# Layer one of a message network inside the stage that counts its edges

## The chip, the cores and the metric

The kernel runs on one core of a Trainium2 chip. Its time is the device time in microseconds (us) of one execution. A core has TensorE (PE in the profile; PEld are its weight loads), VectorE (DVE), ScalarE (ACT), GpSimd (POOL) and SyncE (SP). SP and ScalarE issue the DMAs here, each on a queue of its own.

## The reference, cut to what matters

```python
# N = 3125 nodes, E = 100000 edges sorted by dst, D = 128, 200 relations
deg = jnp.maximum(segment_sum(ones, dst, N), 1.0)
norm = deg ** (-0.5)
h = jnp.maximum(_layernorm(x), 0.0)
for W_r, W_sl, W_el in ((W_r1, W_sl1, W_el1), (W_r2, W_sl2, W_el2)):
    self_msg = jnp.where(isolated[:, None], h @ W_el, h @ W_sl)
    agg = segment_sum((rel_embed[rel_id] + h[src]) @ W_r, dst, N)
    h = rrelu(agg * norm + self_msg)         # slope 0.229 below zero
x = x + h
h = jnp.maximum(_layernorm(x), 0.0)
x = x + graph_attention(h, src, dst, ...)    # softmax over the edges of a node
```

## The kernel before, in words

**Counts instead of edges.** The kernel never gathers rows by edge. It builds `counts`: 27 planes of 3125 target columns. Plane j (0 to 24) holds in row p how many edges lead from node 125j + p to each target; planes 25 and 26 hold the same for the two halves of the relations. A segment sum of h over edges is then a dense product of h with `counts`. Nodes come in 25 blocks of 125.

**Counting, `build_counts`.** The edges are cut into 800 tiles of 125, and four tiles make a group, 200 groups in all. Edges are sorted by target, so a group touches a narrow window of columns only. The groups come in 60 batches (`BATCHES`): 20 of four groups, then 40 of three, with a window width per tile from 2 to 17. For each batch VectorE writes one-hot matrices into one of two halves of a ring: `lo` at line 353, then two builds at line 357. TensorE multiplies them (lines 397 and 399: four tiles of a group, into one of four pairs of PSUM banks) and adds a carried column (line 405, the "carry"). ScalarE takes the next carry out of PSUM (lines 448, 450) and copies the window into `counts` at a column read from a register (line 456); each 20 groups it loads 20 such registers. The last product of a batch frees its ring half (`ring_free`). VectorE waits for the half that TensorE freed, TensorE for `ring_ready`, for its PSUM banks (`put`) and for the carry. Beside it x is normalised in five pieces (statistics on VectorE, the power on GpSimd, lines 261 to 264, the scaling on ScalarE, line 464) and sent to memory as h.

**Checks, `check_counts`.** A stage of its own: degrees by one-column products (line 542), the norm, a check that the columns assumed were right, with a slow second path if not, and the relation rows split into three bf16 parts.

**Layers, `message_layer`.** Twice. First h is split in pieces of five blocks into three bf16 parts (ScalarE lines 871 and 873, VectorE 913 and 915). Then come 13 chunks of two target blocks (the last has one). Per chunk: `own` turns the chunk's own h (line 803), `sums` multiplies 25 blocks by three parts with 250 columns of counts (line 813) and six relation parts (line 816), ScalarE takes both out (877, 879), `weigh` multiplies with the self weights (832) and with W_r (836), ScalarE scales (885) and VectorE finishes (927, 933, 939). Layer two also adds x, stores it, normalises, stores h3, turns it and makes the query rows (lines 822, 841). The last chunk of layer two stores through SP, behind the reload of h3 for attention (lines 757 to 770).

**Attention** follows, and every part (`nc.Block`) ends with a barrier of all engines.

## Time and profile before

| | us |
|---|---|
| median of 3 runs (901.11 to 901.99) | 901.21 |
| the profiled execution | 901.91 |
| its span, first to last instruction | 899.9 |
| counting, to the last window | 0 to 288.6 |
| degrees, checks | 288.6 to 305 |
| layer one | 305 to 446.3 |
| layer two | 446.3 to 591.9 |
| nothing busy | 591.9 to 603.9 |
| attention | 603.9 to 899.9 |

The stages are read from the timeline; the bounds are where TensorE starts or ends the stage's work. The other 2.0 us lie around the span. Busy times are sums over instructions that may overlap on an engine, so an engine near 100% is its stage's limit and one at 60% isn't, unless somebody waits for it each time.

### The profile page before, as it was taken

What the parts mean: (1) busy time and instruction counts of PE and PEld (TensorE: products, weight loads), DVE (VectorE), ACT (ScalarE), POOL (GpSimd) and SP (SyncE); (2) the same over time, 40 slices, a digit from 0 to 9 for tenths busy, and PEclk for the clock granted to TensorE, in tenths of its full rate; (3) what the DMA queues carried; (4) which work ended last, traced back from release to release, by engine and by line L of the source; (5) the groups of instructions that cost most, each with busy time, mean ns of one, the idle gap of its engine ahead of it and who ended that gap; (6) DMA issues with size and microseconds to landing.
All of it is one profiled execution on the core that took longest, in us unless ns stands there. A gap on an engine that the chain in (4) does not pass through costs nothing. (4 is left out here: it accounts for less than half of the span.)

```text
span 899.9 us, 16551 instructions
## 1 busy us (share of the span) xinstructions
PE 740.8 (82%) x5767; PEld 552.3 (61%) x5767; DVE 529.8 (59%) x947; ACT 424.2 (47%) x1019; POOL 242.2 (27%) x248
## 2 busy tenths in 40 slices
PE   4466665666666599999799999929999999999994
PEld 3456555655656498888789999814444444444463
DVE  4998989899996411111343333313458585867677
ACT  0555666567666311111221111117767676767661
POOL 3054920000000000000000000005657666666662
PEclk6555789899899699999899999959999999999996
DMA  4000000000001000000001111120000000000000
GB/s 117 10 3 29 28 17 2 2 2 1 1 1 59 28 1 0 0 0 0 21 19 34 34 37 37 34 91 19 0 1 7 17 9 14 15 10 20 4 23 17
DMA packets 22080, 17.20 MB, mean 19 GB/s; under 512 B 1122, under 2 KB 20224, under 8 KB 22024
## 3 DMA queue, kind: packets, MB, share of 16 engines
q1 hardware_dynamic: 21804, 16.09, 6.1%
q8 instruction: 31, 0.51, 0.2%
q10 hardware_dynamic: 220, 0.40, 0.1%
q14 instruction: 25, 0.20, 0.1%
HBM read 10.09 MB, written 6.40 MB: 18 GB/s over the span
## 5 line engine op out<-in xcount | busy, mean ns | idle before, releaser
L397 PE MATMUL sums<-work 125*128 125x196 f16 (+15 forms) x1220 | 159.2, 265 | 66.6 <-DVE work L357 66.5
L813 PE MATMUL l_ps_g<-counts,work 125*128 (+2 forms) x1950 | 209.0, 269 | 0.6 <-DVE work L915 0.6
L813 PEld LDWEIGHTS l_ps_g<-counts,work 125*128 125x128 bf16 x1950 | 184.9, 99 | 19.0 <-DVE work L915 1.1
L1178 POOL TENSOR_TENSOR counts<-counts,work 125x500 f32<-125x500 f32 x150 | 162.3, 1082 | 97.5 <-DVE work L1242 84.1
L1101 PE MATMUL a_ps_o<-work 125*128 125x500 f32 (+1 forms) x350 | 159.6, 547 | 7.1 <-DVE work L1246 6.1
L1089 PE MATMUL a_ps_s<-work 128*125 128x500 f32 x300 | 152.9, 592 | 12.4 <-PEq L732 12.4
L1242 DVE SCALAR_TENSOR_TENSOR work<-a_ps_s,counts 125x500 f32<-125x500 f32 x150 | 101.5, 677 | 95.0 <-ACT a_ps_s L1198 94.9
L397 PEld LDWEIGHTS sums<-work 125*128 125x128 f16 x1220 | 103.1, 112 | 72.8 <-DVE work L357 71.6
L1193 ACT ACTIVATE a_ps_s<-a_ps_s,work 125x500 f32<-125x500 f32 (+1 forms) x157 | 102.1, 650 | 91.8 <-PE a_ps_s L1089 88.7
L399 PE MATMUL sums<-work 125*128 125x10 f16 (+15 forms) x800 | 138.3, 201 | 0.0
L456 ACT CAST counts<-sums 128x364 f32 (+38 forms) x305 | 130.9, 467 | 8.3 <-issue 1.3
L353 DVE TENSOR_TENSOR work<-work 125x3024 f16<-125x3024 f16 (+1 forms) x60 | 114.1, 1902 | 20.0 <-PE sums L399 18.3
L357 DVE TENSOR_TENSOR work<-work 125x4200 f16<-125x4200 f16 (+15 forms) x120 | 125.4, 1087 | 0.0
L927 DVE SCALAR_TENSOR_TENSOR work<-l_ps_s,small,work 125x128 f32<-125x128 f32 x50 | 15.3, 347 | 171.3 <-ACT work L885 171.3
L1101 PEld LDWEIGHTS a_ps_o<-work 125*128 125x128 f32 x350 | 64.4, 196 | 76.6 <-issue 67.3
L1089 PEld LDWEIGHTS a_ps_s<-work 128*125 128x125 f32 x300 | 55.9, 190 | 78.1 <-issue 78.1
L879 ACT COPY work<-l_ps_g 128x250 f32<-128x250 f32 (+1 forms) x26 | 9.4, 360 | 196.0 <-PE l_ps_g L816 196.0
L1198 ACT ACTIVATE a_ps_s<-a_ps_s,work 125x500 f32<-125x500 f32 (+1 forms) x157 | 100.7, 642 | 0.0
L786 POOL MEMSET work<- 125x1 f32 x1 | 0.1, 98 | 325.3 <-POOLq L732 325.3
L399 PEld LDWEIGHTS sums<-work 125*128 125x128 f16 x800 | 85.6, 108 | 1.6
L405 PE MATMUL sums<-work,ident_h 128*128 128x14 f16 (+2 forms) x305 | 41.3, 187 | 32.0 <-ACT work L448 17.2
L405 PEld LDWEIGHTS sums<-work,ident_h 128*128 128x128 f16 x305 | 25.8, 110 | 38.6 <-ACT work L448 19.8
(157 smaller groups left out, 625.2 us busy)
## 6 DMA issues: line engine op xcount, KB each, us to landing
counts<-in_x SPq DMA_DIRECT2D x5, 312.5 KB
h_nodes<-counts SPq DMA_DIRECT2D x5, 312.5 KB
work<-h_nodes SPq DMA_DIRECT2D x5, 312.5 KB
work<-in_x SPq DMA_DIRECT2D x12, 125.0 KB
x_after_messages<-work SPq DMA_DIRECT2D x12, 125.0 KB
h_attention<-work SPq DMA_DIRECT2D x12, 125.0 KB
work<-h_attention SPq DMA_DIRECT2D x2, 750.0 KB
counts<-x_after_messages SPq DMA_DIRECT2D x12, 125.0 KB
```

Source lines behind the costliest of these rows:

```text
L353: dve.tensor_tensor(lo[:, 0:t * 2 * LO].rearrange("p (t c two) -> p t c two", c=LO // 2, two=2), iota_h[:, None, 0:LO].rearrange("p o (c t ...
L357: last = dve.tensor_tensor(out.rearrange("p t (c two) -> p t c two", two=2), iota_h[:, None, 0:c].rearrange("p o (c two) -> p o c two", tw ...
L397: pe.matmul(win[:, 0:c, cols], lo[:, k * 2 * LO:k * 2 * LO + 128], m[:, k, h0 * w:(h0 + c) * w].rearrange("p (h d) -> p h d", d=w), start= ...
L399: last = pe.matmul(win[:, c:, cols], lo[:, (2 * k + 1) * LO:(2 * k + 1) * LO + 128], r[:, k, :].rearrange("p (h d) -> p h d", d=w), start= ...
L456: act.copy(counts[:, h0:h1, bass.ds(at0, c)], buf[:, i, 0:(h1 - h0) * span].rearrange("p (h d) -> p h d", d=span)[:, :, 0:c]).then_inc(put ...
L813: pe.matmul(ps_g[:, 0:nb * NP], parts[:, j, s, :], counts[0:NP, j, cols], start=j == 0 and s == 0, stop=False)
L1089: last = pe.matmul(out[0:NP, :WIDE], qk_t[:, j * NP:(j + 1) * NP], qk_t[:, c * WIDE:(c + 1) * WIDE], start=True, stop=True)
L1101: last = pe.matmul(ps_o[c % 2][:, 0:cols(u) // n], h3[:, j + i, :], pbuf[u % PB][:, i * NP:i * NP + cols(u) // n], start=j + i == 0, stop= ...
L1178: pool.tensor_tensor(a, a, p, ALU.add).then_inc(acc_done, 1)
L1193: act.activation(s, s, ACT.Relu, bias=five, scale=-float(D) ** -0.5).then_inc(limited, 1)
L1198: act.activation(s, s, ACT.Exp, bias=five, scale=-1.0).then_inc(exped, 1)
L1242: dve.scalar_tensor_tensor(pbuf[u % PB], ps_s[u % 4][0:NP, 0:WIDE], float(np.exp(-CLIP)), counts[0:NP, j, c * WIDE:(c + 1) * WIDE], ALU.ma ...
```

## The change

`build_counts`, `check_counts` and the two calls of `message_layer` become one function, `messages`, in one block. Since the edges are sorted, the first 250 columns of `counts` are final once a certain group is put, and so on: `READY` lists that group for each of the 13 chunks. `plan` gives layer one's steps to slots, a slot being the place between a group's one-hot products and its carry. Chunk 0 begins at group 72, chunk c at `READY[c]` + 3: `own` there (with the degrees of the chunk), eight source blocks (24 matmuls) in each of the next three slots, the last block with `self` and `rest` in the fourth, `agg` two slots on. The chunks begin at 72, 85, 103, 118, 131, 143, 154, 165, 174, 183 and 192; the last two (11 and 12) run behind group 199. The PSUM ring of counting has three pairs of banks, the fourth serves layer one.

To make room, x, the three parts of h and the keys of the one-hot matrices lie in columns of `counts` that aren't counted yet, and move when counting comes near: after chunk 1 SP stores columns 0 to 499 of 25 planes to memory (`heads`), moves late keys and later the parts there, and brings the columns back after the last chunk. h of layer one goes to memory (`store`), and comes back for chunks 0 to 9; chunks 10 to 12 stay. The norm is a power on GpSimd per chunk. The checks move into counting, with new ones that every chunk's columns are final when assumed. Layer two runs its chunks in the order 2 to 11, 1, 0, 12, unrolled. At its end x and h3 of the last chunk are stored from ScalarE's queue, the reload of h3 has six pieces, and attention waits for each piece only where it needs it.

```diff
-             "flag": sb("flag", [1, 1], I32)}
-        T["h3"] = view(T["work"], 4 * N, NP, NB * D, F32)
-        T["hn_in"] = [ctx.enter_context(nc.semaphore(f"hn_in{i}")) for i in range(5)]
-        T["h3_in"] = [ctx.enter_context(nc.semaphore(f"h3_in{i}")) for i in range(3)]
-        build_counts(nc, ctx, T, src, dst, rel, x, h_dram)
-        T["wts1"] = ctx.enter_context(nc.semaphore("weights1_in"))
-        T["rel_step1"] = ctx.enter_context(nc.semaphore("rel_step"))
-        check_counts(nc, ctx, T, src, dst, rel, rel_embed, w_r1, w_sl1, w_el1)
-        message_layer(nc, ctx, T, 1, None, None, None, {})
-        message_layer(nc, ctx, T, 2, w_r2, w_sl2, w_el2, {"x": x, "x2": x2, "h3": h3, "wqk": wqk, "bqk": bqk})
...
+LB = 2
+CHUNKS = -(-NB // LB)
+READY = (58, 82, 100, 115, 128, 140, 151, 162, 171, 180, 189, 197, 200)
+FIRST_SLOT = 72
+AT_ONCE = 8
...
+    for c in range(CHUNKS):
+        s0 = FIRST_SLOT if c == 0 else READY[c] + 3
+        s1 = READY[c + 1] + 1 if c + 1 < CHUNKS else GROUPS
+        s0, s1 = min(s0, GROUPS), min(s1, GROUPS)
+        slots[s0].append(("own", c, 0))
+        for j in range(NB):
+            slots[min(s0 + 1 + j // AT_ONCE, GROUPS)].append(("sum", c, j))
+        s1 = min(s0 + 1 + NB // AT_ONCE, GROUPS)
+        slots[s1].append(("self", c, 0))
+        slots[s1].append(("rest", c, 0))
+        slots[min(GROUPS, s1 + 2)].append(("agg", c, 0))
+    at = {}
+    for g, steps in enumerate(slots):
+        for kind, c, j in steps:
+            at[kind, c] = g
+    assert all(at["agg", c] <= at["own", c + 1] for c in range(CHUNKS - 1))
+    return slots, at
+
...
-            sp.wait_ge(h_out, 16 * 5)
-            sp.wait_ge(ring_free, len(BATCHES) - 1)
-            for i in range(5):
-                sp.dma_start(hn[0:NP, 5 * D * i:5 * D * (i + 1)], h_dram[:, 5 * D * i:5 * D * (i + 1)]).then_inc(T["hn_in"][i], 16)
+            def store(c):
+                sp.wait_ge(y_done, c + 1)
+                sp.dma_start(h1_dram[:, c * LB * D:(c + 1) * LB * D], t1.rearrange("p b f -> p (b f)")).then_inc(h1_out, 16)
+
+            store(0)
+            store(1)
+            sp.wait_ge(sums_done, 2)
+            sp.wait_ge(put, 2 * READY[1])
+            for i in range(5):
+                v = slice(5 * i, 5 * i + 5)
+                sp.dma_start(heads.rearrange("p (j d) -> p j d", d=HEAD)[:, v, :], counts[0:NP, v, 0:HEAD]).then_inc(put_out, 16)
+            sp.wait_ge(put_out, 16 * 5)
+            for b in range(MOVED, len(BATCHES), 4):
+                i = b - MOVED
+                got = counts[0:NP, key_plane(b), KEY_AT:KEY_AT + 8 * KEY_TILES].rearrange("p (a s e) -> p s a e", a=2, s=4)
+                for a in range(2):
+                    sp.dma_start(counts[0:NP, i:i + 4, 3 * D + 48 * a:3 * D + 48 * a + 48], got[:, :, a, :]).then_inc(keys_moved, 16)
+            store(2)
+            for i in range(5):
+                v = slice(5 * i, 5 * i + 5)
+                sp.dma_start(counts[0:NP, v, 0:3 * D], counts[0:NP, v, PART_AT:PART_AT + 3 * D]).then_inc(parts_moved, 16)
+            for c in range(3, DIRECT):
+                store(c)
+            sp.wait_ge(ring_free, len(BATCHES))
+            sp.wait_ge(h1_out, 16 * DIRECT)
+            for i, (j0, j1) in enumerate(PIECES2[:4]):
+                sp.dma_start(hn[0:NP, j0 * D:j1 * D], h1_dram[:, j0 * D:j1 * D]).then_inc(hn_in[i], 16)
+            sp.wait_ge(sums_done, CHUNKS)
+            for i in range(5):
+                v = slice(5 * i, 5 * i + 5)
+                sp.dma_start(counts[0:NP, v, 0:HEAD], heads.rearrange("p (j d) -> p j d", d=HEAD)[:, v, :]).then_inc(heads_in, 16)
...
+                again_sp(sp)
+                sp.wait_ge(R["parts2"], 10)
+
+
+            sp.wait_ge(put, 2 * GROUPS)
+            sp.wait_ge(agg_done, CHUNKS)
+            for t, v in zip((wr, ws[:, 0:D], ws[:, D:]), weights2):
+                sp.dma_start(t, v).then_inc(L["wts"], 16)
+            sp.dma_start(wqk, wqk_d).then_inc(L["wts"], 16)
+            sp.dma_start(bqk, bqk_d.rearrange("(p o) -> p o", o=1)).then_inc(L["wts"], 16)
+            sp.dma_start(x_last, by_block(x, LAST)).then_inc(L["last_in"], 16)
+            sp.wait_ge(y_done, CHUNKS)
+            for i, c in enumerate(ORDER2[:-1]):
...
-                    if g < 4:
-                        pe.wait_ge(later_keys, 3 * (g + 1))
-                    else:
-                        pe.wait_ge(put, 2 * (g - 3))
+            def layer1(kind, c, j):
+                nb = blocks_of(c)
+                p = parts1(c)
+                cols = cells(c)
+                w = nb * NP
+                if kind == "own":
+                    pe.wait_ge(put, 2 * READY[c])
+                    if c:
+                        pe.wait_ge(agg_out, c)
+                    else:
+                        pe.wait_ge(outside_set, 3)
+                        pe.wait_ge(flagged, 1)
+                        pe.wait_ge(rest1[1], 1)
+                    if c == HEAD_CHUNK:
+                        pe.wait_ge(parts_moved, 16 * 5)
+                    for b in range(nb):
+                        for s in range(3):
+                            pe.matmul(ps1[:, h_at + b * NP:h_at + (b + 1) * NP], p[:, c * LB + b, s, :], ident_h[0:NP, 0:NP], start=s == 0, stop=s == 2)
+                    for b in range(nb):
+                        k = c * LB + b
+                        for h in range(RH):
+                            last = pe.matmul(ps1[0:NP, 2 * h_at + b:2 * h_at + b + 1], counts[0:RL, NB + h, k * NP:(k + 1) * NP], ones_h,
+                                             start=h == 0, stop=h == RH - 1)
+                    last.then_inc(own_done, 1)
+                if kind == "sum":
+                    if j == 0:
+                        pe.wait_ge(ht_out, c + 1)
+                    if c == 0 and j % 5 == 0:
+                        pe.wait_ge(rest1[1], j // 5 + 1)
+                    for s in range(3):
+                        pe.matmul(ps1[:, 0:w], p[:, j, s, :], counts[0:NP, j, cols], start=j == 0 and s == 0, stop=False)
+                if kind == "self":
+                    if c == 0:
+                        pe.wait_ge(wts1, 16 * 3)
+                    else:
+                        pe.wait_ge(y_done, c)
+                    for b in range(nb):
+                        last = pe.matmul(ps2[0:NP, b * 2 * D:(b + 1) * 2 * D], ht[:, b * NP:(b + 1) * NP], ws, start=True, stop=True)
+                    last.then_inc(self_done, 1)
+                if kind == "rest":
+                    if c == 0:
+                        pe.wait_ge(rel_step, 6)
+                    for h in range(RH):
+                        for s in range(3):
+                            last = pe.matmul(ps1[:, 0:w], rel_parts[:, h, s, :], counts[0:RL, NB + h, cols], start=False, stop=h == RH - 1 and s == 2)
+                    last.then_inc(sums_done, 1)
+                if kind == "agg":
+                    pe.wait_ge(agg_out, c + 1)
+                    pe.wait_ge(self_taken, c + 1)
+                    for b in range(nb):
+                        last = pe.matmul(ps2[0:NP, b * D:(b + 1) * D], ht[:, b * NP:(b + 1) * NP], wr, start=True, stop=True)
+                    last.then_inc(agg_done, 1)
+
+            for b, (n, w) in enumerate(BATCHES):
...
-                with sp.Fori(1, FULL) as c:
-                    chunk(c, LB)
-                sp.wait_ge(summed, FULL + 1)
-                sp.wait_ge(h3_out, 16 * FULL)
-                reload(0, 0, 12)
-                reload(1, 12, FULL * LB)
-                chunk(FULL, NB - FULL * LB)
-                sp.wait_ge(h3_out, 16 * (FULL + 1))
-                reload(2, FULL * LB, NB)
-                sp.wait_ge(x2_out, 16 * (FULL + 1))
+            sp.wait_ge(L["summed"], CHUNKS)
+            sp.wait_ge(L["h3_out"], 16 * LAST)
+            for i, (j0, j1) in enumerate(T["h3_pieces"]):
+                if j0 == LAST * LB:
+                    sp.wait_ge(L["h3_last"], 16)
+                sp.dma_start(T["h3"][:, j0 * D:j1 * D], h3[:, j0 * D:j1 * D]).then_inc(T["h3_in"][i], 16)
+            sp.wait_ge(L["x2_out"], 16 * LAST)
+            sp.wait_ge(L["x2_last"], 16)
...
+                nb = blocks_of(c)
+                v = slice(c * LB, c * LB + nb)
+                w = nb * NP
+                ps1, ps2 = psum[:, 6, :], psum[:, 7, :]
+                if kind == "own":
+                    deg = ps1[0:NP, 2 * LB * NP:2 * LB * NP + nb]
+                    act.wait_ge(own_done, c + 1)
+                    act.activation(iso[:, v], deg, ACT.Relu, bias=1.0, scale=-1.0).then_inc(iso_set, 1)
+                    act.copy(degs[:, v], deg)
+                    if c:
+                        act.wait_ge(agg_done, c)
+                    act.copy(ht[:, 0:w], ps1[:, LB * NP:LB * NP + w]).then_inc(ht_out, 1)
+                    act.wait_ge(iso_set, 2 * c + 1)
+                    act.activation(some[:, v], iso[:, v], ACT.Identity, bias=1.0, scale=-1.0).then_inc(iso_set, 1)
+                if kind == "self":
+                    act.wait_ge(self_done, c + 1)
+                    act.wait_ge(iso_set, 2 * c + 2)
+                    if c:
+                        act.wait_ge(y_done, c)
+                        act.wait_ge(h1_out, 16 * min(c, DIRECT))
+                    for b in range(nb):
+                        k = c * LB + b
+                        both = ps2[0:NP, b * 2 * D:(b + 1) * 2 * D]
+                        act.mul(t2[:, b, :], both[:, 0:D], some[:, k:k + 1])
+                        last = act.mul(t1[:, b, :], both[:, D:], iso[:, k:k + 1])
+                    last.then_inc(self_taken, 1)
+                if kind == "rest":
+                    act.wait_ge(sums_done, c + 1)
+                    act.copy(ht[:, 0:w], ps1[:, 0:w]).then_inc(agg_out, 1)
+
...
+                if kind in ("own", "self", "rest"):
+                    layer1(kind, q)
+                    if kind == "own" and q == DIRECT + 1:
+                        for i in range(5):
+                            split(i)
+                    if kind == "rest" and q == DIRECT + 2:
+                        split(5)
+            split(6)
+            flag = act.alloc_register("again_act")
+            act.wait_ge(flagged, 1)
+            act.reg_load(flag, T["flag"][0:1, 0:1])
...
+            def ending(c):
+                nb = blocks_of(c)
+                dve.wait_ge(agg_done, c + 1)
+                dve.wait_ge(norm_set, c + 1)
+                if c:
+                    dve.wait_ge(y_done, c)
+                agg = psum[0:NP, 7, 0:LB * D].rearrange("p (b f) -> p b f", f=D)
+                for b in range(nb):
+                    k = c * LB + b
+                    dve.scalar_tensor_tensor(t1[:, b, :], agg[:, b, :], norm[:, k:k + 1], t1[:, b, :], ALU.mult, ALU.add).then_inc(y_step, 1)
+                done = LB * c + nb + c
+                dve.wait_ge(y_step, done)
+                t = t1[:, 0:nb, :]
+                dve.tensor_tensor(t, t, t2[:, 0:nb, :], ALU.add).then_inc(y_step, 1)
+                dve.wait_ge(y_step, done + 1)
+                out = t if c < DIRECT else hn_n[:, c * LB:c * LB + nb, :]
+                dve.scalar_tensor_tensor(out, t, SLOPE, t, ALU.mult, ALU.max).then_inc(y_done, 1)
+
+
...
-                dve.wait_ge(x2_out, c * 16 + 16)
-                dve.memset(rstd[0:1, 0:1], 1.0).then_inc(chunk_done, 1)
+                    rows(i - 1, ORDER2[i - 1])
+            act.wait_ge(L["x2_ready"], CHUNKS)
+            act.dma_start(by_block(x2, LAST), tmp[:, 0:1, :]).then_inc(L["x2_last"], 16)
+            late(LAST, LAST)
+            act.dma_start(h3[:, LAST * LB * D:], x_last.rearrange("p b f -> p (b f)")).then_inc(L["h3_last"], 16)
+            rows(LAST, LAST)
```

Three places in the order of instructions. TensorE, late in counting, between the last products of one group (lines 397, 399; 1021, 1023 after) and the first of the next: before,

```order
L397 MATMUL sums<-work 128x11x17
L399 MATMUL sums<-work 128x2x17
L405 MATMUL sums<-work,ident_h 128x14 [waits carry_ready]
L405 MATMUL sums<-work,ident_h 128x13
L397 MATMUL sums<-work 128x14x17 [waits put,ring_ready]
```

and after, at slot 193, the second slot of chunk 10:

```order
L1021 MATMUL sums<-work 128x11x17
L1023 MATMUL sums<-work 128x2x17
L982 MATMUL sums<-counts 128x250 [waits m_ht_out]
L982 MATMUL sums<-counts 128x250 x23
L1031 MATMUL sums<-work,ident_h 128x14 [waits carry_ready]
L1031 MATMUL sums<-work,ident_h 128x13
L1021 MATMUL sums<-work 128x14x17 [waits put,ring_ready]
```

The burst of 24 matmuls stands ahead of the carry, so ScalarE gets group 193's window later by the burst.

SP's queue from the last count to layer two's first loads: before (h back, then the weights of layer one, then those of layer two),

```order
L217 DMA work<-h_nodes 125x640 [waits ring_free,h_out]
...
L519 DMA work<-in_L0_gnn_rel_embed 100x2x128
L520 DMA work<-in_L0_gnn_W_r1 128x128
...
L737 DMA work<-in_L0_gnn_W_r2 128x128
...
L755 DMA work<-in_x 125x2x128
```

and after:

```order
L582 DMA work<-h_layer_one 125x640 [waits m_h1_out,ring_free]
L582 DMA work<-h_layer_one 125x640 x3
L586 DMA counts<-first_columns 125x5x500 [waits m_sums_done]
L586 DMA counts<-first_columns 125x5x500 x4
L601 DMA work<-in_L0_gnn_W_r2 128x128 [waits m_agg_done,put]
L601 DMA work<-in_L0_gnn_W_sl2 128x128
L602 DMA work<-in_L1_gnn_Wqk 128x128
...
L610 DMA work<-in_x 125x2x128 [waits m_y_done]
```

The return of the first 500 columns now stands in the queue between the last relation sums of layer one and the weights of layer two.

ScalarE behind the last group, after the change only (before, this order is in two blocks, all splits ahead of a layer's chunks):

```order
L1134 COPY work<-sums 128x250 [waits m_agg_done]
L1136 ACTIVATE small<-small 125x2 [waits m_iso_set]
L1212 CAST work<-work 125x5x128 [waits hn_in0]
...
L1212 CAST work<-work 125x5x128 [waits hn_in3]
...
L1212 CAST work<-work 125x2x128 [waits m_y_done]
L1146 ACTIVATE work<-sums,small 125x128 [waits m_y_done,m_h1_out,m_iso_set,m_self_done]
...
L1151 COPY work<-sums 128x250 [waits m_sums_done]
```

The first two rows and the last two belong to chunk 11; the splits of h for layer two (line 1212) stand between them.

## Rows read from the trace of the kernel before

**Rows 1.** Stretches: busy us (instructions) by engine, TensorE clock granted, DMA share, GB/s.

```profile
22.80:106.60 83.80, 49.92 (x648) 43.97 (x648) 77.27 (x125) 49.17 (x176) 37.21 (x17) 0.58 0.05 15
106.60:288.60 182.00, 115.40 (x1677) 106.96 (x1677) 164.44 (x124) 119.98 (x366) 10.85 (x4) 0.90 0.03 9
288.60:305.00 16.40, 5.68 (x52) 5.49 (x52) 4.98 (x18) 3.58 (x5) 0.00 (x0) 0.50 0.23 78
305.00:446.30 141.30, 135.82 (x1229) 121.00 (x1230) 28.67 (x74) 23.89 (x61) 0.10 (x1) 0.98 0.01 2
446.30:591.90 145.60, 140.82 (x1279) 126.95 (x1279) 56.84 (x210) 30.24 (x84) 8.94 (x13) 0.97 0.12 34
591.90:603.90 12.00, 0.00 (x0) 0.02 (x1) 0.06 (x1) 0.07 (x1) 0.03 (x1) 0.50 0.29 115
```

**Rows 2.** Who TensorE waited for, 22.8 to 288.6: us in total, times, longest.

```profile
PE sums L397 <- DVE work L357: 66.5, 46, 4.7
```

**Rows 3.** Timeline of VectorE: start, us, first build of a batch (widths 9, 17).

```profile
123.81 1.73 DVE L353 TENSOR_TENSOR work<-work 125x3024 f16<-125x3024 f16 x1
...
127.12 1.73 DVE L353 TENSOR_TENSOR work<-work 125x3024 f16<-125x3024 f16 x1
...
273.98 1.73 DVE L353 TENSOR_TENSOR work<-work 125x3024 f16<-125x3024 f16 x1
...
278.63 1.73 DVE L353 TENSOR_TENSOR work<-work 125x3024 f16<-125x3024 f16 x1
```

**Rows 4.** Timeline of TensorE: first products of two neighbouring groups, widths 8 and 17.

```profile
114.23 0.25 PE L397 MATMUL sums<-work 125*128 125x200 f16 x1
...
114.82 0.25 PE L397 MATMUL sums<-work 125*128 125x200 f16 x1
...
283.44 0.37 PE L397 MATMUL sums<-work 125*128 125x238 f16 x2 [1.66 <-DVE work L357]
...
284.40 0.27 PE L397 MATMUL sums<-work 125*128 125x238 f16 x1
```

**Rows 5.** Timeline of TensorE in layer one: the sums of two chunks in turn.

```profile
318.45 8.17 PE L813 MATMUL l_ps_g<-counts,work 125*128 x75
...
329.11 8.17 PE L813 MATMUL l_ps_g<-counts,work 125*128 x75
```

**Rows 6.** Timeline of VectorE: the ending of a chunk of layer one.

```profile
329.83 0.61 DVE L933 SCALAR_TENSOR_TENSOR work<-l_ps_a,small,work 125x128 f32<-125x128 f32 x2
330.60 0.42 DVE L939 SCALAR_TENSOR_TENSOR work<-work 125x256 f32 x1 [0.15 <-DVE work L933]
```

**Rows 7.** Timeline: registers reloaded at group 100, and the windows of one group late.

```profile
119.16 0.19 ACT L448 CAST work<-sums 128x27 f16 x1 [3.95 <-issue]
...
120.47 1.73 DVE L353 TENSOR_TENSOR work<-work 125x3024 f16<-125x3024 f16 x1 [2.69 <-PE sums L399]
...
286.16 1.09 ACT L456 CAST counts<-sums 128x504 f32 x2
```

**Rows 8.** Groups of instructions by line: busy us, mean ns of one, idle before.

```profile
L915 DVE TENSOR_TENSOR work<-work 125x640 bf16<-125x640 f32 x10 | 8.3, 826 | 7.9 <-ACT work L873 7.9
```

**Rows 9.** Timeline of TensorE: the last carry, and the first weighing of layer two.

```profile
286.24 0.20 PE L405 MATMUL sums<-work,ident_h 128*128 128x14 f16 x2
...
458.08 1.03 PE L832 MATMUL l_ps_s<-work 128*125 128x256 f32 x4
```

**Rows 10.** Timeline of GpSimd: two of its four steps on the scales of x.

```profile
102.64 11.33 POOL L261 TENSOR_SCALAR counts<-counts 125x5 f32<-125x5 f32 x1 [1.67 <-DVE counts L340]
114.05 1.20 POOL L262 TENSOR_TENSOR counts<-counts 125x5 f32<-125x5 f32 x1
```

**Rows 11.** Stretch while x arrives in pieces of 512 bytes: clock, DMA share, GB/s.

```profile
10.00:24.00 14.00, 0.50 0.37 97
```

**Rows 12.** Timeline at layer two's end: DMAs issued by SP, VectorE's last wait.

```profile
587.88 0.68 SPq L763 DMA_DIRECT2D work<-h_attention  x2
...
588.61 0.33 SPq L757 DMA_DIRECT2D x_after_messages<-work  x1
...
602.63 0.06 DVE L967 MEMSET work<- 1x1 f32 x1 [12.73 <-DMA x_after_messages<-work]
```

1165 lines of the change are left out of this document (642 added, 523 removed).

## The prediction

> **What bounds the kernel now.** I read the stages first, in the table of stretches [rows 1]. The learner is to see two kinds of stage. In the counting stage (22.8 to 288.6) VectorE is busy 92% and 90% of the time and TensorE 60% and 63%; nearly all of TensorE's longest waits there are for VectorE's one-hot batches, 66.5 us in all [rows 2]. In the two message layers (305 to 446.3 and 446.3 to 591.9) TensorE is busy 96% and 97%, VectorE 20% and 39%. Between them lie 16.4 us of counting degrees and checks, and 12.0 us before attention in which nothing computes at all. So layer one's matmuls would fit into TensorE's idle time only where that is large enough: it idles 182.0 - 115.4 = 66.6 us in the second part of counting, and layer one needs 12.5 times 10.66 us [rows 5]. That is the whole case: about 118 us of work go into a hole of 67 us, and what replaces the lost stage must be counted batch by batch.
>
> **Sum, part 1: counting up to group 72.** VectorE sets this pace and gets more to do. From the stage that goes away it takes the split of the relation rows (2.3 us of its 4.98 us of busy time in 288.6 to 305), and 8 of the 10 splits of h in pieces of five blocks (0.83 us each, as they take in the layers [rows 8], so 6.6 us), about 1.2 us of new checks, and up to 5 us for the 25 powers on GpSimd, done at once where five took 1.2 us [rows 10]; I take 2. ScalarE's norms and roundings come closer together (+1). Some of it falls into pauses VectorE has anyway (2.7 us at the worst one [rows 7]), -2. Sum +11 us, bounds 7 to 16. TensorE reaches group 72 at 117.7 instead of 106.7.
>
> **Part 2: groups 72 to 199.** A batch of three groups costs VectorE 3.31 us at width 9 and 4.65 us at width 17 [rows 3]; over the 42 batches that is 168 us, and pauses make it 180 (106.7 to 286.4). A group costs TensorE 0.59 us at width 8 and 0.96 us at width 17 [rows 4], 97 us in all by interpolation. Eleven of the thirteen chunks are placed here. A chunk is 10.66 us [rows 5], plus four one-column matmuls for the degrees, 118 us. Bare sums say TensorE 215 us, VectorE 168 plus eleven endings of 1.8 us (two steps at 0.61 a pair, two at 0.43 and the waits between them [rows 6]) = 188 us. But the one-hot ring holds one batch ahead only, so VectorE can't save up work during a burst: each batch costs the larger of the two. I added up the batches so. 23 of them hold bursts and are TensorE's: 55 us of counting and 107 us of layer one, and 28 us of waits that the change adds, 2.5 us a chunk: the turned h (ScalarE copies it after a carry of 0.2 us, evictions of 1.1 us for a group [rows 7] and two small steps, while TensorE has one group of 0.96 us to do), and the same way round before `agg`, where ScalarE has four products and a copy, 1.8 us, in front. The other 19 batches stay VectorE's: 83 us. Together 273 us. VectorE starts its next batch before the burst behind a batch's last group: -9. The reload of places each 20 groups (ScalarE silent 3.95 us, VectorE 2.69 [rows 7]) costs +5, since some fall into bursts. So 269 us for 180: +89, bounds +70 (no added waits) and +108 (4 us a chunk). Last group at 117.7 + 269 = 386 instead of 286.4: **+100 us** with part 1.
>
> **Part 3: from the last group to layer two's first products.** Before, the last count was done at 286.4 and the first `weigh` of layer two began at 458.1 [rows 9]: 171.7 us. After, two chunks are left, 10.7 and 6 us. ScalarE's order puts the splits 0 to 4 ahead of chunk 11's products: h comes back 12 us after the last group (1.28 MB; [rows 11] for the rate), and the last split ends at about +16, so `agg` of chunk 11 is at +18 and not +13, and the last relation sums are at +24. Own and sums of layer two (0.3 and 8.8 us) follow, ready to weigh at +35. Here is the step that I think matters most: at +24 SP issues the return of 500 columns of 25 planes, 3.1 MB, and only behind it, in the same queue, the weights of layer two. One queue moved 97 GB/s in pieces of 512 bytes and 115 GB/s in pieces of 6 KB [rows 11, 1], so 27 to 32 us, I take 29, and 4 to 5 for the weights and landing: they are there at +58. That a small transfer really waits behind a big one in that queue is seen at layer two's end: the last store of x, issued at 588.61 behind 1.5 MB, released VectorE at 602.63 [rows 12]. So layer two weighs at +58, not +35: saved 171.7 - 58 = **114 us**, bounds 137 (no such stall) and 110. The stall lets the clock drop to half, as the idle stretch ahead of attention does (0.50 granted [rows 1]); I put **+2 us** on the way back up, about four microseconds at half speed.
>
> **Part 4: end of layer two.** Layer two itself keeps its chunks, in another order, 145.6 us of which 2.5 were waiting for the first parts; that gain is inside the 171.7. The 12 us at its end are the store above. In the change this store and the last h3 go through ScalarE's queue and attention waits piece by piece, so the stage should end some 2 us after the last h3: **-10 us**, bounds 0 (it waits all the same) and -11. No row of before shows a small transfer on the second queue beside a large one on the first. The Trainium skill (DMA: Bandwidth & Descriptors, Queues, rings and completion order) says that descriptors of one ring are taken in ring order, and that a DMA engine takes turns between queue rows; the first agrees with [rows 12], the second no run shows yet, and by the two of them the weights stall stands and this gain is whole. Attention stays at 296 us.
>
> **Sum**: 899.9 + 100 - 114 + 2 - 10 = 878 us of span. The profiled run took 901.9 us for a span of 899.9, the median is 901.2, so **879 us**.
>
> **Rivals.** (a) The weights do not wait: heads move at twice the rate, or the queue lets them by. 23 us less, 856. Against it is the 14 us of [rows 12]. (b) The bursts cost less: ScalarE's copies hide behind the group beside them and the waits of 2.5 us vanish, 861. For it: each burst sits between a group and its carry, where TensorE had waits anyway. (c) **Slower, by the clock.** TensorE pauses while it waits for ScalarE or an empty ring, and in counting, where it pauses most, it is granted 0.58 before 106.6 and 0.90 after it [rows 1]. Layer one ran at 0.98. If more than a fifth of the 118 us of burst work runs at half speed, 24 us are added and the gain is gone: 903 to 906. Against it: bursts are long and dense, and behind a pause of 1.66 us the group at 283.44 still took 0.96 us [rows 4], which is the full clock. (d) GpSimd computes the norms: one of its small steps took 11.33 us beside VectorE's one-hots and ended in a pause of VectorE [rows 10]. A VectorE-bound batch with an ending would wait for it, 1 us each and +8 in the whole, 887. The Trainium skill (SBUF — State Buffer, on the shared port pair) has a rule that speaks against this placing: the pair is locked for a whole instruction and the other engine blocks. By it the norm is late wherever VectorE has no pause; between `own` and `agg` bursts give it one, and an ending that waits makes one itself. (e) The queue again: heads out (28 us), 4000 pieces of keys, the move of parts (24 us) and the stores of layer one's results share SP's queue. I get the third result out some 10 us before ScalarE needs its buffer, the fourth 8 us before. If keys take twice what I give them TensorE stands for 10 us: 889. (f) Attention starts no earlier: 888. (g) The change doesn't do what it says: if the new checks (every chunk's columns final at its group) find the data outside, the second path runs, and the time is many times this.
>
> **How the numbers follow.** Forecast 0.43; (a) 0.14; (b) 0.12; (c) 0.10; (d) 0.06; (e) 0.08; (f) 0.06; (g) 0.01. The forecast's own range is 868 to 890. The range for 8 in 10 goes from (a) to just short of (c): 855 to 902. A measurement can tell 0.2%, 1.8 us. Faster by more: all but (c), (g) and the upper edge of the others, 0.86; within: 0.03; slower: 0.11.
>
> **What would show it.** Right: the last counting matmul near 386; TensorE over 90% busy in 118 to 386 with VectorE at about 70%; in layer two a first `weigh` near +58 with nothing busy for about 20 us ahead of it and the bytes of the return moving meanwhile; TensorE in attention within 3 us of layer two's end. Wrong: the counting stage ends outside 370 to 400; no pause ahead of the first `weigh`; a granted clock under 0.9 in the bursts; ScalarE waiting for `m_h1_out` at chunks 3 or 4.

## The result, and the profile after

The changed kernel takes **913.5 us** (median of 4 runs, 912.8 to 914.2), the kernel before beside it 901.6 us (4 runs, 901.1 to 902.0): a ratio of 1.013, with a 95% interval of 1.0115 to 1.015. It is slower, by 1.3%; the forecast was 879 us. The profiled execution has a span of 912.4 us, for 899.9 us before.

The stages of the changed kernel, to set beside [rows 1]: each line is a stretch and its length, then busy us (and instructions) of PE, PEld, DVE, ACT, POOL, the granted clock of TensorE, the DMA share, and GB/s.

```profile
22.80:120.70 97.90, 52.83 (x668) 46.11 (x669) 87.29 (x142) 55.95 (x192) 10.62 (x3) 0.55 0.09 25
120.70:415.50 294.80, 236.41 (x2739) 213.95 (x2739) 179.61 (x165) 136.99 (x454) 27.52 (x22) 0.90 0.09 26
415.50:445.00 29.50, 19.41 (x203) 17.49 (x200) 11.24 (x21) 12.69 (x34) 2.44 (x7) 0.88 0.14 48
445.00:475.40 30.40, 11.46 (x87) 9.54 (x87) 1.25 (x5) 2.61 (x5) 0.00 (x0) 0.68 0.36 115
475.40:609.00 133.60, 129.94 (x1189) 118.16 (x1189) 50.06 (x202) 24.26 (x73) 8.93 (x13) 0.98 0.13 36
609.00:616.40 7.40, 1.11 (x3) 0.64 (x3) 0.00 (x0) 0.63 (x2) 0.00 (x0) 0.53 0.32 122
```

The second line is the news. Layer one went into counting as meant, and TensorE works 236 us there, but the stretch has 295 us: TensorE is busy 80%, VectorE 61%. Neither is full. Of whom TensorE waited for from 117 to 416 (us in total, times, longest), to set beside [rows 2]:

```profile
PE sums L1031 <- ACT work L1186: 21.9, 5, 8.2
PE sums L1021 <- DVE work L829: 14.6, 11, 2.0
PE sums L1002 <- ACT work L1151: 11.1, 11, 1.2
PE sums L982 <- ACT work L1134: 7.7, 10, 1.2
PE sums L1031 <- ACT work L1184: 4.5, 1, 4.5
```

Before, over the same groups (103.9 to 286.2), TensorE waited 48.2 us for VectorE's batches and 18.8 us for carries. Now it is 14.6 us for the batches (line 829), and 26.4 us in six waits for the carry that ScalarE copies (lines 1184 and 1186). The other 18.8 us (lines 982 and 1002) are the waits at the bursts. In ScalarE's timeline those copies stand behind silences of its own, in which it waited for nothing that a semaphore shows ("issue"). Each is a load of 20 places, as in [rows 7]. The two longest, in groups 100 and 120, with what VectorE and TensorE did beside the second:

```profile
181.38 0.18 ACT L1186 CAST work<-sums 128x28 f16 x1 [7.53 <-issue]
...
221.00 1.73 DVE L823 TENSOR_TENSOR work<-work,counts 125x3024 f16<-125x3024 f16 x1 [3.66 <-PE sums L1023]
...
231.46 0.18 ACT L1186 CAST work<-sums 128x28 f16 x1 [13.37 <-issue]
231.70 0.23 PE L1031 MATMUL sums<-work,ident_h 128*128 128x14 f16 x2 [8.17 <-ACT work L1186]
```

And SP's transfers in that stretch, by their issue (start, us until the queue had taken them):

```profile
166.33 21.08 SPq L566 DMA_DIRECT2D first_columns<-counts  x5
200.58 6.81 SPq L572 DMA_DIRECT2D counts<-counts  x8
...
208.23 18.19 SPq L576 DMA_DIRECT2D counts<-counts  x5
```

Both long silences lie beside large moves that the change brings: the first (173.9 to 181.4) beside the heads going out, the second (218.1 to 231.5) beside the parts; 105 and 106 GB/s move in them. The other four behind group 72 last 2.9 to 4.4 us. Two ahead of it last 6.0 and 5.6 us (ending at 81.8 and 107.6), and 53 and 55 GB/s move there.

The milestones, from the timelines (start of the last carry product for a group, of the first `weigh` of layer two, of attention's first product; us):

| kernel | group 71 | group 199 | weigh | attention | span | median |
|---|---|---|---|---|---|---|
| before | 103.9 | 286.2 | 458.1 | 603.9 | 899.9 | 901.6 |
| changed | 117.2 | 416.2 | 475.4 | 617.4 | 912.4 | 913.5 |
| e1_spread | 116.5 | 400.5 | 457.1 | 598.8 | 893.9 | 894.6 |
| e2_weights | 117.0 | 412.8 | 455.5 | 609.1 | 904.3 | 906.0 |
| e3_nomove | 117.3 | 399.7 | 441.4 | 581.2 | 875.8 | 878.6 |
| e4_reg4 | 108.7 | 383.2 | 441.6 | 583.6 | 878.8 | 882.4 |
| e7_return | 116.3 | 409.3 | 451.1 | 592.4 | 887.0 | 893.3 |
| e8_end | 117.1 | 415.4 | 475.2 | 613.9 | 912.5 | 912.7 |
| e9_all | 109.1 | 366.3 | 404.4 | 541.2 | 835.8 | 842.9 |

The milestones of e7_return and e9_all are those of their fastest executions, 888.7 and 837.5 us, so they lie some 5 us under the medians beside them.

One more thing makes the stretch long, and the waits don't show it. Four of these kernels have the same instructions from group 71 to 199: the changed one, e2_weights, e7_return and e8_end. The stretch took 299.0, 295.8, 293.1 and 298.4 us, with TensorE busy 239.1, 233.7, 229.3 and 236.0 us. The changed kernel and e7_return:

```profile
117.17:416.18 299.01, 239.09 (x2767) 216.40 (x2766) 183.79 (x170) 138.42 (x459) 27.52 (x22) 0.90 0.09 25
116.26:409.32 293.06, 229.27 (x2767) 209.55 (x2766) 184.18 (x171) 138.36 (x459) 25.59 (x22) 0.94 0.09 26
```

TensorE's clock has two levels, 1.2 GHz (granted 0.50) and 2.4 GHz. In windows of 0.2 us the changed kernel is at the lower one for 62 us of this stretch, in nine spells, one at each of the six silences; e7_return is for 38 us, e9_all for 19. An estimate of what that takes: in slices of 1 us, TensorE's busy time times one minus the granted clock. With it, TensorE's time from group 71 to 199 is accounted for (us):

| kernel | span | work at the full clock | lost to the clock | waits for carries | at bursts | for VectorE's batches |
|---|---|---|---|---|---|---|
| changed | 299.0 | 216.3 | 22.8 | 26.4 | 18.8 | 14.6 |
| e7_return | 293.1 | 217.2 | 12.1 | 27.1 | 19.5 | 17.1 |
| e1_spread | 284.1 | 215.6 | 14.6 | 27.0 | 17.7 | 9.1 |
| e3_nomove | 282.4 | 216.8 | 14.3 | 15.5 | 18.9 | 16.7 |
| e4_reg4 | 274.6 | 217.0 | 14.4 | 7.5 | 21.1 | 14.5 |
| e9_all | 257.2 | 216.1 | 8.0 | 6.4 | 17.5 | 9.1 |

The work at the full clock comes out the same in all six, within 1.6 us, which speaks for the estimate. Not all that the clock takes is the kernel's: between the first two rows 10.7 us of it go with 5.9 us of the span.

### The profile page after: what moved, and what is told of

Read it like the earlier page. It is cut to its first block and busy times, and to the rows that moved or that the text cites. A ratio compares the mean times of both kernels' runs of the same rounds, so it can differ in the third digit from the quotient of the medians.

```text
span 912.4 us, 15380 instructions
## 1 busy us (share of the span) xinstructions
PE 744.3 (82%) x5767; PEld 554.2 (61%) x5767; DVE 526.8 (58%) x931; ACT 428.6 (47%) x1085; POOL 242.1 (27%) x273
## 5 line engine op out<-in xcount | busy, mean ns | idle before, releaser
L1021 PE MATMUL sums<-work 125*128 125x196 f16 (+15 forms) x1220 | 162.3, 265 | 39.9 <-DVE work L829 39.9
L823 DVE TENSOR_TENSOR work<-work,counts 125x3024 f16<-125x3024 f16 (+1 forms) x60 | 114.3, 1905 | 108.2 <-PE sums L1023 101.0
L829 DVE TENSOR_TENSOR work<-work,counts 125x4200 f16<-125x4200 f16 (+15 forms) x120 | 125.5, 1087 | 0.0
L982 PE MATMUL sums<-counts 125*128 125x250 f16 (+1 forms) x975 | 113.6, 275 | 10.0 <-ACT work L1134 10.0
L672 POOL TENSOR_SCALAR work<-work 125x2 f32<-125x2 f32 (+1 forms) x13 | 15.4, 1187 | 355.5 <-ACT work L1134 355.5
L982 PEld LDWEIGHTS sums<-counts 125*128 125x128 bf16 x975 | 92.4, 101 | 21.3 <-ACT work L1134 11.9
L1061 PE MATMUL sums<-counts,work 125*128 125x250 f16 (+1 forms) x975 | 104.8, 270 | 0.0
L1061 PEld LDWEIGHTS sums<-counts,work 125*128 125x128 bf16 x975 | 93.2, 99 | 8.9
L1186 ACT CAST work<-sums 128x28 f16 x104 | 20.1, 193 | 126.2 <-PE sums L1031 94.9
```

The costliest lines, as they stand in the source:

```text
L823: dve.tensor_tensor(lo[:, 0:t * 2 * LO].rearrange("p (t c two) -> p t c two", c=LO // 2, two=2), iota_h[:, None, 0:LO].rearrange("p o (c t ...
L829: last = dve.tensor_tensor(out.rearrange("p t (c two) -> p t c two", two=2), iota_h[:, None, 0:c].rearrange("p o (c two) -> p o c two", tw ...
L982: pe.matmul(ps1[:, 0:w], p[:, j, s, :], counts[0:NP, j, cols], start=j == 0 and s == 0, stop=False)
L1021: pe.matmul(win[:, 0:c, cols], lo[:, k * 2 * LO:k * 2 * LO + 128], m[:, k, h0 * w:(h0 + c) * w].rearrange("p (h d) -> p h d", d=w), start= ...
L1061: pe.matmul(ps_g[:, 0:w], parts[:, j, s, :], counts[0:NP, j, cells(c)], start=j == 0 and s == 0, stop=False)
```

## Experiments

Medians are of 4 to 10 runs; the kernel before beside them took 901.3 to 902.0 us in every group of runs. "Changed" is 913.5 us.

**1. e1_spread.** Is it true that a batch costs the larger of two parts, so that bursts are cheaper when spread?

```diff
-AT_ONCE = 8
+AT_ONCE = 4
```

> The changed kernel with four source blocks behind a group instead of eight, so a chunk's sums stand behind seven groups and not four. Theory A (the one-hot ring holds one batch ahead, so each batch costs the larger of TensorE's and VectorE's part): the same batch-by-batch sum that gave 272 us for groups 72 to 199 now gives 255, so the last group comes 18 us earlier and the kernel takes 895 us (888 to 900). Rival B (TensorE's work and its stalls at register loads and moves simply add up, wherever the sums stand): within 3 us of 913. Rival C (the small waits multiply, one behind each group instead of one behind each burst): slower, 918 to 925.

894.6 us (890.7 to 897.1), ratio to before 0.991 (0.988 to 0.994): theory A's range. Groups 72 to 199 took 284.1 us instead of 299.0, 15 less for 17 forecast (272 to 255), with ScalarE silent 3.2 us longer in all than in the changed kernel. But the batch model of part 2 is not shown by this size. It says that spreading saves waits for VectorE's batches, and those fell by 5.5 us only; 8.2 us of the 15 are clock, by the table above. Beside e7_return, whose clock is nearer, the stretch is 9.0 us shorter, 8.0 of it waits for batches. So the direction holds, rival B and C are out, and the size was met in part by the clock.

**2. e4_reg4.** What does a load of places cost?

```diff
-            CHUNK = 20
+            CHUNK = 4
```

> The changed kernel with ScalarE loading the places of 4 groups every 4 groups instead of 20 every 20. Theory A (a load costs by the register, some 0.2 us each): ten silences of 3 to 13 us become fifty of 0.6 to 1 us, which TensorE's three groups of PSUM cover, and the last group comes 15 to 25 us earlier: 893 us (888 to 898). Rival B (a load costs 2.5 us and more however many registers): ScalarE is silent for 125 us and more, a part of it on the way of the carries: slower, 935 to 1000. In between (half of the cost fixed): 905 to 915.

882.4 us (880.5 to 883.2): theory A, and more than it said. ScalarE's silences behind carries fall from 50.9 us (nine) to 17.6 us (fifteen over 0.3 us), 33.3 us less, and the last group comes 33.0 us earlier. That the two agree is in part chance. Up to group 72, where VectorE sets the pace, 12.7 us less silence gave 8.5 us. Behind it 20.7 us less silence gave 24.4 us: TensorE waited 18.9 us less for carries, and 8.4 us less went to the clock. Two ordinary loads of four, and the first of those beside a move, in ScalarE's timeline:

```profile
131.75 0.18 ACT L1184 CAST work<-sums 128x27 f16 x1 [0.58 <-issue]
...
156.65 0.18 ACT L1184 CAST work<-sums 128x27 f16 x1 [0.52 <-issue]
...
164.29 0.18 ACT L1186 CAST work<-sums 128x28 f16 x1 [3.58 <-issue]
```

The last one stands where the heads go out: even four registers then take 3.6 us, and 3.8 us once more beside the parts (ending at 208.5). The Trainium skill (Runtime: NRT & Kernel Launch, Instruction fetch mechanics) gives about 200 ns a register for a load of registers, in a remark on those at launch, which it says are read from HBM. Here the values lie in SBUF. The silences of 20 that have at most 31 GB/s beside them, 2.8 to 4.4 us, are 0.14 to 0.22 us a register, near that figure; those beside more traffic are longer.

**3. e6_before4.** Do small loads help the kernel before as much?

```diff
-            CHUNK = 20
+            CHUNK = 4
```

> The kernel before with ScalarE loading the places of 4 groups every 4 groups, as in e4_reg4. There ScalarE was silent 33.3 us less and the last group came 33 us earlier, since TensorE, which waits for it, set the pace. Theory A (in the kernel before VectorE sets the pace and idled about 2.7 us at each of nine silences; small loads give that back): 15 to 22 us faster, 883 us (879 to 887), so cheap loads help the changed kernel 10 to 15 us more than the kernel before. Rival B (VectorE's time is used anyway, the silences are hidden in the kernel before): 898 to 902. Rival C (they help both alike): 868 to 872.

889.7 us (889.6 to 889.9), 0.9865 of before (0.985 to 0.988): between A and B, 11.6 us where A said 15 to 22. ScalarE's silences behind carries, those over 0.3 us, fell by 18.8 us (36.5 to 17.6) and the last group came 12.2 us earlier (274.0 for 286.2): 0.65 us for each, as in the changed kernel up to group 72 (8.5 for 12.7), where it gains 1.2 behind it (24.4 for 20.7). So a silence costs less where VectorE sets the pace. Five of the small loads there still kept ScalarE silent for 2.1 to 2.5 us (at 71.7, 83.6, 99.1, 111.9 and 126.0); why those is open.

**4. e3_nomove.** Are the two long silences made by the moves?

```diff
-   ...[:, v, :], counts[0:NP, v, 0:HEAD]).then_inc(put_out, 16)
+   ...[:, 5 * i, 0:64], counts[0:NP, 5 * i, 0:64]).then_inc(put_out, 16)
```

(the return of the heads and the move of the parts in the same way; the kernel leaves out most of both copies and so computes with wrong data, but its instructions are the same)

> The changed kernel, where the saving and the return of the head columns and the move of the split h copy only 64 columns of 5 planes instead of everything (chunks 6 to 12 and layer two thus compute with wrong data, the instructions are the same). Theory A (ScalarE's register loads are served beside the data transfers and wait for them): its silences of 7.5 and 13.4 us at groups 100 and 120 fall to 3 to 4 as at the other loads, groups 72 to 199 take 13 to 16 us less, and with the stall at the weights gone (another 15) the kernel takes 883 us (880 to 887). Rival B (the silences have to do with something else at these groups): only the stall at the weights goes, 896 to 899, and the silences stay.

878.6 us (877.5 to 882.6): theory A. In the timeline of ScalarE in this kernel the silences of groups 100 and 120 are

```profile
178.71 0.18 ACT L1186 CAST work<-sums 128x28 f16 x1 [4.77 <-issue]
...
217.70 0.18 ACT L1186 CAST work<-sums 128x28 f16 x1 [3.81 <-issue]
```

12.3 us less than 7.53 and 13.37, the other seven are as in the changed kernel within 0.1 us. The last group comes 16.5 us earlier; groups 100 to 139, in which they lie, took 80.5 us for 94.8. The first `weigh` stands 41.8 us behind the last group instead of 59.3, without a wait. So a register load is slowed by data transfers that no semaphore ties it to. By which path was not tried. The gain is more than the silence, since TensorE's clock lost 8.5 us less here.

**5. e5_three.** The changed kernel's counting has three pairs of PSUM banks, not four. Alone in the kernel before:

```diff
-                        pe.wait_ge(put, 2 * (g - 3))
+                        pe.wait_ge(put, 2 * (g - 2))
...
-  2 * (g % 4) + i
+  2 * (g % 3) + i
```

> The kernel before with three pairs of PSUM banks in the counting ring instead of four, as the changed kernel has them. Theory A (TensorE gets only one group ahead of ScalarE anyway, since it waits for the next carry behind each group's products, so the fourth pair covers nothing): within 2 us of before, 900 to 904. Rival B (the fourth pair lets TensorE work through ScalarE's silences at the register loads, and its loss is part of why counting is longer in the changed kernel): slower by 5 to 12 us, 906 to 913.

901.33 us against 901.30 of before, ratio 0.9999 (0.999 to 1.001): theory A: in the kernel before, the fourth pair covers nothing. Whether it would where TensorE sets the pace, in the changed kernel, was not tried.

**6. e2_weights.** Do the weights wait only for what is ahead of them in their queue?

```diff
+            act.wait_ge(agg_done, CHUNKS)
             for t, v in zip((wr, ws[:, 0:D], ws[:, D:]), weights2):
-                sp.dma_start(t, v).then_inc(L["wts"], 16)
+                act.dma_start(t, v).then_inc(L["wts"], 16)
```

> The changed kernel with layer two's weights, wqk, bqk and the last rows of x issued by ScalarE's queue as soon as layer one's last products are taken, and not by SP's behind the return of the head columns. Theory A (a transfer waits behind what its own queue was given before, and only that): the weights land within 5 us, the 16.4 us that TensorE stands ahead of layer two's first weigh fall to at most 2, and the kernel takes 898 us (896 to 901). Rival B (the 16 DMA engines are full with the return, so a second queue gets in no sooner): within 3 us of 913. Between them: the two queues share evenly, the weights need twice their time, 901 to 904.

906.0 us (905.7 to 910.7), ratio to before 1.006: theory A's mechanism, not its sum. The wait of 16.35 us ahead of the first `weigh` went, and 11.0 us, two thirds of it, came back one step on. Of the 7.5 us gained, about 5 are this; in the profile the last group came 3.4 us earlier, without a changed instruction ahead of it. In this kernel, by timelines of TensorE and VectorE:

```profile
473.51 0.43 DVE L910 TENSOR_TENSOR work<-work 125x256 f32<-125x256 f32 x1 [14.50 <-DMA work<-in_x]
...
476.96 0.65 PE L1065 MATMUL sums<-work 125*128 125x125 f32 x2 [11.02 <-DVE work L924]
```

VectorE waits for the first rows of x, which SP issues behind the heads' return, and TensorE for what VectorE makes of them. I had taken one transfer out of the queue where two were needed.

**7. e7_return.** Take the large transfer away instead:

```diff
+                if i < 8:
+                    v = slice(3 * i, 3 * i + 3 if i < 7 else NB)
+                    sp.dma_start(counts[0:NP, v, 0:HEAD], heads...[:, v, :]).then_inc(heads_in, 16)
```

> The changed kernel, where the head columns come back in eight pieces, one behind the stores of each of layer two's first eight chunks, so that layer two's weights and its first rows of x are issued with nothing ahead of them. In e2_weights the weights alone went ahead, TensorE's 16.4 us at them went, and 11.0 us came back as a wait for the first rows of x, which stood in the same queue behind the return. Theory A (the return in one piece is the whole of both stalls, and a piece of 0.4 MB fits into the 5 us between a chunk's last store and the next load): 897 us (895 to 899), no wait above 4 us at layer two's first weigh. Rival B (the pieces delay the loads of x in each of the eight chunks by 1 to 3 us, and that comes back): 903 to 912.

893.3 us (888.7 to 895.1), ratio to before 0.991 (0.990 to 0.993): theory A's mechanism, 2 us better than its range. The return gives 17.5 us of it; the profile has 6.9 us more ahead of the last group, where no instruction differs and TensorE's clock lost 12.1 us for 22.8. The first `weigh` stands 41.8 us behind the last group, as in e3_nomove, and from there to layer two's last product it takes 134.2 us, for 135.1 in the changed kernel: eight pieces between the chunks' transfers delayed nothing.

**8. e8_end.** What holds the end of layer two?

```diff
-            for i, (j0, j1) in enumerate(T["h3_pieces"]):
+            for i, (j0, j1) in enumerate(T["h3_pieces"][:1]):
```

(the other five pieces first in attention's block)

> The changed kernel, where only the first of the six pieces of h3 is loaded before attention's block begins, and the other five are the first things that SP issues in it. Theory A (the block ends late since SP needs 10.0 us to issue six pieces one behind the other, 606.8 to 616.8, while TensorE is done at 610.5): attention begins 4 to 5 us earlier and nothing is late behind it, 908.5 us (907 to 910). Rival B (the pieces then come late where attention uses them): 911 to 915. Rival C (the two last stores on ScalarE's queue hold the block's end by themselves): attention begins at most 2 us earlier, 911 to 913.

912.7 us (912.2 to 914.3): rival B in its sum. In the changed kernel TensorE waited 6.94 us for the block's end, and SP's issue of the six pieces began at 606.81 and took 10.04 us:

```profile
606.81 10.04 SPq L620 DMA_DIRECT2D work<-h_attention  x6
...
617.42 1.17 PE L1377 MATMUL a_ps_s<-work 128*125 128x500 f32 x1 [6.94 <-PEq L536]
```

In e8_end attention began at 613.87, 3.6 us earlier (0.8 of it already at the last group), behind a wait of 3.35 us instead of 6.94: the issue of the pieces held it, for 3.6 us of the wait. What the other 3.35 us are is open. But then

```profile
629.47 0.22 DVE L1597 COPY work<-work 128x125 f32<-128x125 f32 x1 [4.29 <-DMA work<-in_L_gnn_beta]
```

stood for attention's six small loads, now behind five pieces of h3 in the queue. It is the same mistake as in e2_weights, one stage on.

**9. e9_all.** AT_ONCE 4, four registers a load, the return in eight pieces, and the end of e8_end with the small loads ahead of the five pieces.

> The changed kernel with what the runs so far point to, together: four source blocks behind a group (e1_spread), four registers a load (e4_reg4), the head columns back in eight pieces behind layer two's chunks (e7_return), and only the first piece of h3 loaded ahead of attention's block, the other five in it but behind attention's six small loads, since in e8_end VectorE stood 4.3 us for those behind the five pieces, which cost what the earlier begin of attention had won. Theory A (the four causes are separate places of the time, and only the first two share some TensorE idle time, of which I take off 4): 913 - 31 - 19 + 4 - 17 - 4 = 846 us (841 to 853). Rival B (less silence leaves less to fill, so four blocks at once instead of eight give nothing more): 860 to 865. Rival C (the end stays as in e8_end): 4 us more than A.

**842.9 us** (837.5 to 845.1), ratio to before 0.936 (0.934 to 0.938): theory A. The single gains, added up as above, come 3 us from it; no run paired them two by two. Its stretch from group 72 to 199 and the one to the first `weigh`:

```profile
110.00:366.50 256.50, 224.09 (x2762) 205.62 (x2762) 182.46 (x167) 139.14 (x453) 32.64 (x22) 0.96 0.11 30
366.50:404.40 37.90, 29.69 (x281) 25.58 (x281) 12.33 (x25) 14.55 (x39) 2.67 (x7) 0.91 0.14 47
```

TensorE is busy 87% in the first, for 80% in the changed kernel, VectorE 71% for 61%. Ahead of attention it waits 2.92 us, and nothing is late in it. Against the kernel before with small loads alone (889.7 us) the changed structure, its own stalls mended, is worth 47 us.

**10 to 12. GpSimd beside VectorE.** The changed kernel is 10.7 us late at group 8 (44.2 for 33.5), where VectorE makes the checks and all 25 statistics in one lump. e10_stats spreads the statistics, five blocks behind each of the batches 1 to 5:

```diff
-                if b == 1:
-                    statistics()
+                if 1 <= b <= 5:
+                    statistics(b - 1)
```

> As e9_all, and the statistics of x on VectorE in five pieces behind the batches 1 to 5 instead of all behind batch 1. Theory A (TensorE stands for the lump, but VectorE, which sets the pace up to group 72, has the same sum of work either way, so the time of group 72 does not move): within 2 us of e9_all. Rival B (the 10 us by which the changed kernel is later at group 8 are the lump itself, and group 72 comes 5 to 10 us earlier without it): 5 to 10 us less than e9_all.

848.5 us (847.0 to 849.0), 5.6 us slower than e9_all: neither. Group 8 came 5.1 us earlier and group 71 5.6 us later, since VectorE waited 4.64 us behind batch 6 for GpSimd's powers, which began later. e11_late takes them behind batch 8:

```diff
+                if b == 8:
                     dve.wait_ge(root_x, 1)
```

> As e10_stats, but VectorE takes GpSimd's 25 powers behind batch 8 instead of batch 6. In e10_stats the spread statistics let GpSimd begin 15.6 us later (56.55 for 40.94), and VectorE stood 4.64 us for its powers behind batch 6, which with 1 us of more small steps is the 5.6 us by which it was slower than e9_all. Theory A (VectorE's sum of work sets the time of group 72; the lump costs nothing, the wait was all of the loss): group 72 within 1.5 us of e9_all's 109.1 and the time within 2.5 us of e9_all's 842.9. Rival B (something else of the spreading costs, such as TensorE's or ScalarE's order behind it): the 5.6 us stay, 848 to 849. Rival C (without the wait the spread statistics win, since VectorE no longer finds the ring full early on): 836 to 839.

845.4 us (843.6 to 846.8): inside A's range, but not by A's reason. Group 71 came at 114.1, not at 109.1 within 1.5, for VectorE still waited 4.2 us. And e12_relations:

```diff
-                if b == 3:
+                if b == 6:
                     relations()
```

> As e11_late, and VectorE splits the relation rows (2.3 us of small casts and subtractions) behind batch 6 instead of batch 3. In e11_late GpSimd's power over 25 columns took 10.91 us (59.81 to 70.72) and ended 4.2 us after VectorE's last one-hot build had ended, whereas it took 4.35 us in e10_stats, where VectorE stood still beside it, and 4.42 us in e9_all, where it began beside the split of the relation rows and went on beside one-hot builds. Theory A (VectorE's one-hot builds, one right behind the other, keep a step of GpSimd from beginning, but not from going on): the power begins beside the split, takes 4.3 to 4.6 us, VectorE's 4.2 us of waiting behind batch 8 go, group 72 comes at 110 instead of 114.1, and the time is 841 us (839 to 844). Rival B (a step of GpSimd advances only while VectorE builds no one-hots): the split gives it 2.3 us, VectorE still waits 2 us, group 72 at 112, 843 us. Rival C (the power simply takes 11 us beside anything of VectorE's): 11 us again, and a wait of 1 to 3 us.

843.8 us (842.4 to 844.3), group 71 at 109.7: theory A. What decides is the power's own time, since B's 843 us lies as near. With it the three runs are back at e9_all (842.9 us, group 71 at 109.1): spreading the statistics won nothing. GpSimd's power of 25 columns in e10_stats, e11_late and e12_relations:

```profile
59.81 4.35 POOL L666 TENSOR_TENSOR counts<-counts 125x25 f32<-125x25 f32 x1
```

```profile
59.81 10.91 POOL L666 TENSOR_TENSOR counts<-counts 125x25 f32<-125x25 f32 x1
```

```profile
57.62 4.42 POOL L666 TENSOR_TENSOR counts<-counts 125x25 f32<-125x25 f32 x1
```

The first ran while VectorE stood still. The second met one-hot builds back to back and ended 4.2 us after the last of them. The third began beside the split of the relation rows (57.1 to 59.4) and went on beside one-hot builds from 59.52 at no loss to either. The Trainium skill (SBUF — State Buffer, SBUF: two separate sides) says that of a VectorE instruction with two inputs in SBUF, as the builds are, and a GpSimd one that reads SBUF, whoever starts first holds the pair of ports which they share for its whole instruction, and the other blocks. The runs agree for GpSimd as the second comer, though it stood through six builds in a row and not through one; for VectorE as the second comer they don't: its build at 59.52 in e12_relations took 2.26 us, as everywhere.

## Why the prediction was wrong, step by step

The account, from the milestones, forecast and measured:

| step | forecast | measured |
|---|---|---|
| part 1, to group 72 | +11 | 117.2 - 103.9 = +13.3 |
| part 2, groups 72 to 199 | +89 | 299.0 - 182.3 = +116.7 |
| part 3, last group to `weigh` | -114 | 59.3 - 171.8 = -112.6 |
| layer two, clock on the way up | +2 | 135.1 - 133.5 = +1.6 |
| part 4, end of layer two | -10 | 6.9 - 12.3 = -5.4 |
| attention | 0 | -1.0 |
| sum | -22 | +12.6 |

**Part 2 is the step that failed**, outside its bounds of +70 to +108, and two of its terms did it: what the register loads cost, and the clock. Its sum was 269 us: 215 of TensorE's work, 28 of waits at bursts, and by difference 26 for all waits for VectorE and the loads. The table of TensorE's time has 216 of work, 19 at bursts, 41 for batches and carries, and 23 lost to the clock, together 299.

The first is the term "the reload of places each 20 groups costs +5, since some fall into bursts". It took the silence of 3.95 us and VectorE's 2.69 us in [rows 7], and counted only what a reload costs more than before. But where TensorE sets the pace it waits for the carry through most of the silence: the six in the stretch last 35.2 us together (4.37, 7.53, 13.37, 4.12, 2.96 and 2.85), and TensorE stood 26.4 us at them. Two of them were not 4 but 7.5 and 13.4 us, made longer by the change's own moves. e4_reg4 showed that smaller loads take most of this away (24.4 us less in the stretch), e3_nomove that the moves make it longer (12.3 us less silence, 16.5 us less time). I had looked at these moves, in rival (e), but only for who waits for their data, not for who shares their path.

The second is that the sum priced all of TensorE's work in part 2 at the full clock, and kept the half clock for rival (c). No run holds the clock fixed; the account above and the four kernels with the same instructions are what there is on it. By the changed kernel and e7_return some 0.55 us of each microsecond that it takes from TensorE are the kernel's (5.9 for 10.7), so about 13 of the 23 us, an estimate.

The idea that each batch costs the larger of its two parts is borne out in direction by e1_spread, not in size. The waits at bursts were 9 us less than the sum had. The credit of 9 us for VectorE's head start I can't find in any run.

**Part 1** was right within its bounds. Part of it is again silence: with small loads group 71 comes at 108.7, 8.5 us earlier.

**Part 3** was right in mechanism and nearly in size: a pause ahead of the first `weigh`, at +59 for +58, while 115 GB/s move. The pause was 16.35 us and not 23: TensorE was ready 8 us later than forecast (the last sums ended at 26.5 and not 24, and `own` of layer two waited 3.9 us for the last split), and that fell into the pause. Rival (a) is out: e7_return and e3_nomove are what it would have looked like, 17 us less.

**Part 4** got half. That small stores on ScalarE's queue are not held by SP's was right: TensorE waited 6.9 us instead of 12.3. "Some 2 us after the last h3" overlooked that issuing 1.6 MB in six pieces took SP itself 10 us, and the block ends no sooner than its issues.

**The rivals.** (b) is half true and hidden: the waits at bursts were 18.8 us and not 28. (c), the clock, named something real, and the argument against it was wrong. It looked at a pause of 1.66 us; behind the longer ones, at its register loads, the kernel before already ran at the lower level, as behind the load that ended at 228. In the changed kernel it is the same behind all six; its line below stands after the silence of 13.4 us, in which TensorE stood for 8.17 us. The kernel before and the changed one:

```profile
228.10:233.60 5.50, 5.30 (x51) 4.84 (x52) 3.57 (x4) 4.70 (x14) 0.00 (x0) 0.50 0.00 0
231.60:237.00 5.40, 5.30 (x33) 4.29 (x34) 0.00 (x0) 1.64 (x7) 0.00 (x0) 0.50 0.09 27
```

Such a spell costs TensorE about 2.7 us of work, and all of them together 22.8 us, of which by the estimate above some 13 are the kernel's. (c) had 24 us, for the bursts alone; here the bursts and the counting products share the loss. Up to group 72 the clock doesn't matter: the changed kernel was granted 0.55 there, e1_spread, with the same instructions, 0.95, and e8_end 1.00, and group 71 came at 117.2, 116.5 and 117.1. (d), GpSimd: not in the chunks, where the norm took 1.2 us on average and no ending of layer one waited for it, but in the 25 powers, as the last three runs show. (e): ScalarE waited for no result's store; the queue hurt by another way. (f): no. (g): no.

The range ended at 902 because I gave the upper side to a single mechanism of known size. The forecast rested on an engine at the limit of its reach, TensorE, having no stall that belonged to a third engine, and [rows 7] showed one.

## What to carry to other kernels

When a change moves the bound from one engine to another, list the stalls of the third engine again: a silence that cost two thirds of itself before cost more than all of itself here, once the waiting engine set the pace and its clock fell behind each. Where the trace of before shows the half clock behind such stalls, price the work behind them at it. Before a transfer is taken out of the way of a large one in its queue, list everything that is issued behind it; moving or cutting the large one is the surer edit. And load registers in small portions where a copy with its place in a register stands in a chain of carries.
